# Attention values loaded by ScalarE's queue instead of SyncE's

## The reference

```python
xn = _rms(x, g1)
Q, K, V = (xn @ Wq.T, xn @ Wk.T, xn @ Wv.T)   # each (b, s, 16 heads, 16)
pQ = jax.nn.elu(Q); pK = jax.nn.elu(K)
Q1, Q2 = jnp.split(pQ, 2, axis=-1); K1, K2 = jnp.split(pK, 2, axis=-1)
kv1 = jnp.einsum('bshe,bshd->bsed', K1, V) * SCALE    # contracted over the heads of one token
kv2 = jnp.einsum('bshe,bshd->bsed', K2, V) * SCALE
attn = jnp.einsum('bshe,bsed->bshd', Q1, kv1) - lmb * jnp.einsum('bshe,bsed->bshd', Q2, kv2)
attn = (1.0 - LAMBDA_INIT) * _rms(attn, g2)
attn = _rms(attn.reshape(b, s_len, E), g3) + attn
```

## Time and profile before

| what | value |
|---|---|
| median of 3 runs | 917.29 us (915.17 to 919.27) |
| the profiled execution | 918.34 us |
| its span | 916.7 us |
| mean granted TensorE clock | 0.958 |
| attention loop on TensorE | 517.2 to about 626 us |
| one iteration of it without `turn_heads` | 2.94 us |
| one iteration with `turn_heads` | 3.38 us |

### The profile page before, as it was taken

How to read it: one execution, slowest core, us unless ns; L and a number is a source line. 1 busy time by engine, 2 the same in 40 slices (tenths; PEclk the granted TensorE clock), 3 DMA queues, 4 the chain that set the end, 5 groups by cost and what they waited for, 6 DMA issues and landing times. The chain is left out here.

```text
span 916.7 us, 23149 instructions
## 1 busy us (share of the span) xinstructions
PE 824.3 (90%) x8838; PEld 685.8 (75%) x8838; DVE 613.7 (67%) x1405; ACT 482.3 (53%) x999; POOL 254.7 (28%) x323
## 2 busy tenths in 40 slices
PE   5999999999799999998999899989989749999960
PEld 4788888887577777766677688776667739999960
DVE  2567787777547777777555335778776875757626
ACT  2444444443677777766964335554754314445325
POOL 1156554212112222223000000013332041646344
PEclk9999999999999999999999899999999759999995
DMA  8500000000000000002587344334222212556439
GB/s 307 190 25 18 23 17 18 22 11 2 2 1 1 1 2 1 1 1 69 127 197 183 94 132 132 109 121 146 93 93 93 92 34 99 150 170 179 121 53 344
DMA packets 74637, 79.55 MB, mean 87 GB/s; under 512 B 21824, under 2 KB 65728, under 8 KB 74176
## 3 DMA queue, kind: packets, MB, share of 16 engines
q1 hardware_dynamic: 69584, 72.36, 25.8%
q0 software_dynamic: 3968, 5.25, 3.3%
q10 hardware_dynamic: 1008, 0.91, 0.3%
HBM read 50.70 MB, written 27.79 MB: 86 GB/s over the span
## 5 line engine op out<-in xcount | busy, mean ns | idle before, releaser
L712 DVE TENSOR_TENSOR r_prob<-r_pS,const 128x512 f32<-128x512 f32 x128 | 82.0, 682 | 25.1 <-PE r_pS L539 25.1
L1088 DVE SCALAR_TENSOR_TENSOR f_gl<-att_res,small_first,f_gh 128x512 fp32r<-128x512 f32 x64 | 47.3, 748 | 37.1 <-ACT f_gh L1013 34.8
L942 PE MATMUL f_pY<-wpjT,f_gh 128*128 128x256 f32 x256 | 66.1, 292 | 0.4 <-DVE f_gl L1088 0.4
L943 PE MATMUL f_pY<-wpjT,f_gl 128*128 128x256 f32 x256 | 63.4, 281 | 0.0
L1356 PEld LDWEIGHTS q_bank<-q_xT,att_res 128*64 128x64 f32 x1024 | 55.6, 137 | 7.2 <-issue 4.2
L942 PEld LDWEIGHTS f_pY<-wpjT,f_gh 128*128 128x128 f32 x256 | 48.7, 190 | 15.9 <-issue 13.4
L2426 POOL DMA_INDIRECT sum_dram<-e_yo,y_id x24 | 43.1, 1796 | 63.0 <-ACT e_yo L2559 47.2
L1356 PE MATMUL q_bank<-q_xT,att_res 128*64 128x128 f32 x1024 | 59.2, 274 | 0.0
L1007 ACT ACTIVATE att_res<-f_pH 128x512 f32<-128x512 f32 x64 | 38.1, 595 | 40.0 <-PE f_pH L927 39.3
L2540 ACT ACTIVATE e_hh<-e_pH 128x320 fp32r<-128x320 f32 x64 | 26.2, 434 | 55.1 <-PE e_pH L2465 54.9
L838 POOL TENSOR_SCALAR t_ey<-t_es 128x8 f32<-128x8 f32 x4 | 0.8, 202 | 188.6 <-ACT t_sqrow L1911 188.6
(11 more groups left out here) (305 smaller groups left out, 2380.7 us busy)
## 6 DMA issues: line engine op xcount, KB each, us to landing
kv_dram<-att_res SPq DMA_DIRECT2D x32, 256.0 KB, 3.3
t_ring<-kv_dram SPq DMA_DIRECT2D x128, 64.0 KB, 2.3
wi<-L_ffn_wi SPq DMA_DIRECT2D x8, 1024.0 KB, 5.0
wo<-L_ffn_wo SPq DMA_DIRECT2D x8, 1024.0 KB, 7.6
x_res<-L_attn_x SPq DMA_DIRECT2D x8, 512.0 KB, 5.4
q_dram<-att_res SPq DMA_DIRECT2D x16, 256.0 KB, 3.4
t_q<-q_dram SPq DMA_DIRECT2D x8, 512.0 KB, 3.8
x_dram<-x_res SPq DMA_DIRECT2D x8, 512.0 KB, 3.0
```

What stands on the lines that cost most here:

```text
L712: dve.tensor_tensor(prob[t % 2][:, r, :, :], pS[r][:, :, :], dec[:, r, :, :], ALU.mult)\
L942: pe.matmul(out, gh[c % 4][:, cols], net.wpjT[:, c, :], start=(c == 0 and t % 2 == 0), stop=False, skip_group_check=True)
L943: mm = pe.matmul(out, gl[c % 4][:, cols], net.wpjT[:, c, :], start=False, stop=(c == NH - 1), skip_group_check=True)
L1088: dve.scalar_tensor_tensor(out=gl[c % 4][:, :], in0=g[c][:, :], scalar=net.lnw[:, c:c + 1], in1=gh[c % 4][:, :], op0=ALU.mult, op1=ALU.sub ...
```

## The change

`load_diagonal` takes the queue that issues it and the groups to load. SyncE keeps the queries and keys of chunks 2 to 7. The values of chunks 1 to 7 are issued by ScalarE: groups 0 to 3 at the head of iteration 4m, groups 4 to 7 at the head of iteration 4m + 1, each ahead of `take_scores`. Both places wait for the queries of chunk m to have landed and for the last scores of chunk m - 1.

```diff
-def load_diagonal(net, sp, part, m, i):
+def load_diagonal(net, queue, part, m, i, groups):
     runs = HEADS // RUN
-    for j in range(GROUPS):
+    for j in groups:
         ...
-        sp.dma_start(net.ring[i % RING][j * HD:(j + 1) * HD, j * runs:(j + 1) * runs, :], src).then_inc(net.ring_in[i % RING].sem, 16)
+        queue.dma_start(net.ring[i % RING][j * HD:(j + 1) * HD, j * runs:(j + 1) * runs, :], src).then_inc(net.ring_in[i % RING].sem, 16)
 ...
-def load_values(net, sp, m):
-    load_diagonal(net, sp, 1, m, 2 * m + 1)
+def load_values(net, queue, m, groups=range(GROUPS)):
+    load_diagonal(net, queue, 1, m, 2 * m + 1, groups)
 ...
     def _(sp):
-        for m in range(1, CHUNKS):
-            if m >= 2 and m % 2 == 0:
+        for m in range(2, CHUNKS):
+            if m % 2 == 0:
                 ...
-            if m >= 2:
-                sp.wait_ge(a_made.sem, a_made.after(SETS * (m - 1)))
-                load_queries(net, sp, m)
-                sp.wait_ge(o_made.sem, o_made.after(SETS * (m - 1)))
-                load_keys(net, sp, m)
-            sp.wait_ge(a_made.sem, a_made.after(SETS * m))
-            load_values(net, sp, m)
+            sp.wait_ge(a_made.sem, a_made.after(SETS * (m - 1)))
+            load_queries(net, sp, m)
+            sp.wait_ge(o_made.sem, o_made.after(SETS * (m - 1)))
+            load_keys(net, sp, m)
 ...
         for n in range(ALL + 2):
+            if SETS <= n < ALL and n % SETS < 2:
+                m = n // SETS
+                act.wait_ge(net.q_in[m % 2].sem, net.q_in[m % 2].after(16 * (m // 2 + 1)))
+                act.wait_ge(a_made.sem, a_made.after(SETS * m))
+                load_values(net, act, m, range(GROUPS // 2 * (n % SETS), GROUPS // 2 * (n % SETS + 1)))
             if n < ALL:
                 take_scores(n)
```

More of the change, by code:

```diff
@@ L1498, in load_queries @@
     sp.dma_start(net.q[m % 2][:, :, :], src).then_inc(net.q_in[m % 2].sem, 16)
-def load_diagonal(net, sp, part, m, i):
+def load_diagonal(net, queue, part, m, i, groups):
     runs = HEADS // RUN
-    for j in range(GROUPS):
+    for j in groups:
         first = ((m // 2 * GROUPS + j) * P + m % 2 * HALF) * RUN
         src = net.kv_dram[part].rearrange("(a p) t -> p a t", p=HD)[:, :, first:first + HALF * RUN]
-        sp.dma_start(net.ring[i % RING][j * HD:(j + 1) * HD, j * runs:(j + 1) * runs, :], src).then_inc(net.ring_in[i % RING].sem, 16)
+        queue.dma_start(net.ring[i % RING][j * HD:(j + 1) * HD, j * runs:(j + 1) * runs, :], src).then_inc(net.ring_in[i % RING].sem, 16)
 def load_keys(net, sp, m):
-    load_diagonal(net, sp, 0, m, 2 * m)
-def load_values(net, sp, m):
-    load_diagonal(net, sp, 1, m, 2 * m + 1)
+    load_diagonal(net, sp, 0, m, 2 * m, range(GROUPS))
+def load_values(net, queue, m, groups=range(GROUPS)):
+    load_diagonal(net, queue, 1, m, 2 * m + 1, groups)
 def attention_mlp_and_route(net, ctx):
```

## The result

The changed kernel took 938.62 us in the median of four executions, against 916.23 us for the kernel before. One of the four took 1393.09 us at a granted clock of 0.554; without it they lie at 932.86 to 939.00, and the median is 938.23. The ratio is 1.022, with a 95% interval of 1.017 to 1.027. Timed again later beside the experiments it was 1.019 (1.016 to 1.023). The change makes the kernel slower, as forecast, but by 18 to 22 us and not by 8: the time lies above my range of 919.5 to 931.0.

A forecast was written before the change was run, and what follows sets the result against it. The loop was taken as bound by TensorE's own matmuls, with DMAs hidden. Late values 6.6 us, plus long issues 2.1, less 0.5 for the keys, gave +8.2 us: 925.5 us, range 919.5 to 931.0.

The forecast's parts named there:

- The place of the loss: Attention loop: mixes of chunks 3, 5 and 7 wait for values some 1, 3 and 3 us; no new cost elsewhere.
- Chunks 4 and 6: Values behind the square root come 1.2 us late in chunk 4, chunk 6 alike; VectorE's waits cover it, cost nothing.
- the landing of 2.3 us: Time from ScalarE's last issue of a chunk's values to their landing, taken as 2.3 us in every chunk.
- The lateness itself: Values landing after the mix wants them in chunks 3, 5 and 7: 1.0 + 2.8 + 2.8 = 6.6 us.
- taking turns at issuing: Rival, chance 0.04: SyncE's and ScalarE's queues hinder each other, +3.5 us in chunks 5 and 7, 929.0 us.
- Long issues: Some of ScalarE's value issues take about 1.0 us more; 0.7 us for each of three sets, 2.1 us.
- The keys' 1.0 us: TensorE's wait before chunk 2's scores: half of it, 0.5 us, won because no values are issued behind the keys.
- The clock: Rival, chance 0.15: stalls in chunks 5 and 7 lower TensorE's clock, 3.7 us more, 929.2 us.

The follow-up runs named there:

- e6: Changed kernel, but the values of chunks 3, 5 and 7 stay on SyncE at their old gates; 918.98 us, ratio 1.001 to the kernel before.
- e3: Changed kernel, but SyncE's keys and expert weights both wait until the values have landed; 926.95 us, ratio 1.011 to the kernel before.
- e1: Changed kernel, but SyncE issues the expert weights only after chunk 7's values have landed; 927.55 us, ratio 1.012 to the kernel before.
- e2: Changed kernel, but SyncE issues the keys of chunk m only after the values of chunk m - 1 have landed; 933.77 us, ratio 1.019 to the kernel before.
- e9: Kernel before, but chunk 2's keys are issued by both queues, groups 0 to 3 by SyncE, 4 to 7 by ScalarE; 916.37 us, ratio 0.998.
- e7: Changed kernel, but TensorE does the scores of set 22 five times and of set 30 eight times; 936.96 us, ratio 1.022 to the kernel before.
- e5: Changed kernel, but ScalarE issues all eight groups in one piece at the head of iteration 4m; 927.19 us, ratio 1.010 to the kernel before.
- e10: e1 with TensorE doing the scores of set 22 five times and of set 30 three times; 926.32 us, ratio 1.009 to the kernel before.
- e8: The control: the changed kernel, unedited, timed again beside the other runs; 935.95 us, ratio 1.019 to the kernel before.

## Why the prediction was wrong

**The place of the loss: right.** Chunks 3, 5 and 7 wait for values, 1, 2, 4 and 6 do not (e6). ScalarE's issues take 0.448 us, and the arrears in chunks 5 and 7 are there.

**Chunks 4 and 6: right for another reason.** I had their values 1.2 us late and the delay covered by VectorE's waits. No cover was needed. In the changed kernel the mix of chunk 4 started at 567.31 without a wait, and VectorE's waits behind it were still 1.66 and 2.98 us. I had put the second piece behind the end of the square root, which stands ahead of it in ScalarE's program. The timeline of ScalarE has the piece beside the root's table load, and the root itself only at 564.47, behind it:

```profile
562.62 0.81 ACTq L1507 DMA_DIRECT2D t_ring<-kv_dram  x2
563.17 1.28 ACT L1897 ACT_TABLE_LOAD   x1
563.46 0.93 ACTq L1507 DMA_DIRECT2D t_ring<-kv_dram  x2
```

**The term that failed: the landing of 2.3 us.** It was the step that carried the miss: the three landings took 3.5, 4.4 and 7.6 us. I took 2.3 us from rows of one queue that issued these small DMAs one after another, and used it where a second queue issues at the same time. I can split each wait by the time at which the mix could have started (its start less its wait) and ScalarE's last issue:

| | mix ready | start of last issue | late with 2.3 us | predicted | landing beyond 2.3 | wait |
|---|---|---|---|---|---|---|
| chunk 3 | 553.58 | 551.59 | 0.3 | 1.0 | 1.2 | 1.5 |
| chunk 5 | 583.15 | 583.25 | 2.4 | 2.8 | 2.1 | 4.5 |
| chunk 7 | 620.24 | 619.36 | 1.4 | 2.8 | 5.3 | 6.7 |

The lateness itself is 4.1 us, where I had 6.6, and e3 measures 4.2. One reason that the rows show is that a piece starts beside ScalarE's last calculation, about 0.5 us early each time in chunk 5; in chunk 3 the second piece began at 550.28, ahead of the squaring of 550.42 which I had put before it. The other 8.6 us are the landings. Chunk 7's 5.3 is the weights: without them its landing took 2.31 us (e1). Those of chunks 3 and 5 are the keys: without them both took 2.22 us (e2). The prediction spoke of SyncE's keys in the same time, but only as a matter of taking turns at issuing, with 0.04; it never listed what SyncE issues next, and so missed the 4 MB. SyncE issues the weights once chunk 6's last mix is made, which TensorE does in iteration 29, and ScalarE issues chunk 7's second piece in that same iteration. In the kernel before, chunk 7's values were out at 607 us and the weights followed at 614.27.

**Long issues** were there (1.33 us in chunk 5's first piece, 1.13 in chunk 3's; none over 0.70 in chunk 7), but in the first pieces. ScalarE went on behind them without a gap, so they moved the second pieces and are part of the 4.1 us of lateness. What they cost can be estimated in chunk 5: in e2 its first piece had no long issue and lasted 1.75 us in place of 2.62, and by the sum of the table it was 1.9 us late in place of 2.4. That is 0.5 us, where I counted 0.7 for each of three chunks, on top of 6.6.

**The keys' 1.0 us stayed.** I had put half of it on values issued behind them. With none behind them the wait was 1.00 again. Its cause stays open: it was gone in e9, where two queues share the issues, but also in e7, where one queue has them all.

**The clock** was a rival at 0.15, worth 3.7 us, and came true. Behind the waits of 4.5 and 6.7 us it was low, in both profiles of the changed kernel. The two falls cost 2.1 and 1.4 us, 3.5 together; a third, behind VectorE's wait of 2.98 us, cost 1.6. The forecast had nothing for them. The clock was tied to the first error: behind waits of 1.94 (e1's chunk 7), 1.82 (e2's chunk 5) and 1.61 us (e3's chunk 7) no fall followed, while behind 2.32 (e3's chunk 5) and 2.77 (e5's chunk 7) one did.

**What made the profiled execution look better.** The 4.8 us before the loop and the 2.5 at its start are stretches of low clock that the profile of before happened to have. Its granted clock was 0.93 in the first 50 us and 0.98 from 200 to 300 us, where the changed kernel's was 1.00 in both. The control is slow in the first 50 us again, also at 0.93, its first scores took 2.82 us, and its time is closer to the median.

## What to carry to other kernels

Before a DMA is moved later in time, list everything that every queue issues in its new slot, and above all the big transfers whose gate is close: a landing time read from a quiet slot does not hold there. On an engine that also calculates, an issue's place in the program counts for more than its cost. And a long wait on TensorE is to be priced with a fall of its clock behind it: here all six waits for values of 4.3 to 6.9 us had one, and the falls priced above cost 1.4 to 2.1 us on top of the wait.

## What the runs showed of the hardware

A DMA issue on ScalarE can begin before the calculation ahead of it has ended: at 577.14 against 577.59 in chunk 5. It can begin even before that calculation has begun: at 562.62 in chunk 4, where the table load and the root that stand ahead of it started at 563.17 and 564.47. The calculation behind a piece came after it: in chunk 5 the score copies started at 579.87 and 583.80, 0.1 us after the last issues had ended.

TensorE can stop with nothing to wait for. In e7 it sat idle for 3.34 us in the middle of matmuls that wait for no other engine, with the DMA engines full of the weights. The stretch of that time:

```profile
624.00:627.00 3.00, 0.00 (x0) 0.00 (x0) 0.00 (x0) 0.00 (x0) 0.00 (x0) 1.00 1.08 349
```

That it was the fetch of instructions is argued, not shown: the wait vanished in e10, where the weights came later, but there were fewer repeats too. The page of the profile counts instruction fetches as DMA queues of their own (q8 and q14). In the kernel before, the nine issues of SyncE in the loop that took over 1.2 us each began within 0.2 us of a fetch by q8, and so did the six of over 1.1 us on both queues in the changed kernel. Whether the fetch is what makes an issue long is not tested. One of the nine stands in the DMA view of 600.1 to 601.8 us, where an issue at 600.23 took 1.49 us:

```profile
q8 instruction: 1, 0.02, 4.2%
```

Behind the longer wait for VectorE (2.8 to 3.1 us, in iteration 27) the clock fell in seven profiles (the changed kernel and e2 to e7) and not in the five others (before, e1, e8, e9, e10), with the same code behind it; in e1 and e8 a low stretch came even behind the shorter one, of 1.6 and 1.8 us. So the length of a wait alone does not decide it here. Such falls are part of the spread of all these runs.
